# A graph network on one core: VectorE's order in the first two steps of a pair is changed

## The reference, cut to what matters

```python
h = x
for i in range(L):                                   # L = 4 layers
    hw = jnp.einsum('bnc,cd->bnd', h, weight[i])
    m = jnp.einsum('bjn,bjd->bnd', adj, hw)          # aggregation over the graph
    h = _gru_cell(m, h, w_ih[i], w_hh[i], b_ih[i], b_hh[i])
return layernorm(x + h * mask)                       # over the 128 channels
# _gru_cell: r, z = sigmoid(xr + hr), sigmoid(xz + hz); n = tanh(xn + r * hn)
#            h = (1 - z) * n + z * h
```

## Time and profile before

| what | value |
| --- | --- |
| median of 3 runs | 537.22 us (536.68 to 537.37) |
| the profiled execution: its own time | 537.31 us |
| its span from first to last instruction | 535.5 us |
| PE busy | 514.2 us, 96% of the span |
| DVE busy | 388.8 us, 73% |
| ACT busy | 383.8 us, 72% |
| POOL busy | 219.9 us, 41% |
| mean granted TensorE clock | 0.988 of full |

### The profile page before, as it was taken

The page is one execution under the profiler, slowest core; times in us unless marked ns, Lnnn a source line. Parts: engine busy times, 40 slices in busy tenths (PEclk is TensorE's granted clock), DMA queues, the critical chain, the costliest instruction groups (busy, mean ns, idle before and its releaser), DMA issues.

```text
span 535.5 us, 7420 instructions
## 1 busy us (share of the span) xinstructions
PE 514.2 (96%) x2288; PEld 422.0 (79%) x2288; DVE 388.8 (73%) x678; ACT 383.8 (72%) x638; POOL 219.9 (41%) x162
## 2 busy tenths in 40 slices
PE   5999999999999999999999999999999999999970
PEld 4688888888888888888888888888888888888760
DVE  3787666666788886666689886667688887767595
ACT  4668777648776779956786877984986777985444
POOL 2045232344345454432336644332355454344443
PEclk9999999999999999999999999999999999999995
DMA  8951653265642356273662166356472165424212
GB/s 305 380 199 47 226 195 126 87 169 156 234 141 80 121 179 226 88 224 119 203 239 77 61 211 215 118 163 190 133 280 80 60 218 171 171 89 151 86 60 82
DMA packets 78896, 85.13 MB, mean 159 GB/s; under 512 B 3768, under 2 KB 61712, under 8 KB 78864
## 3 DMA queue, kind: packets, MB, share of 16 engines
q1 hardware_dynamic: 78864, 84.73, 47.9%
HBM read 64.27 MB, written 20.45 MB: 158 GB/s over the span
## 4 chain that ended last, share of the span: by engine, by line
PE 91%; SPq 2%; DMA 1%; POOL 1%; DVE 1%; issue 1%; ACT 1%; POOLq 0%; DVEq 0%; ACTq 0%
PE p_S L508 40%; PE p_r L522 5%; PE p_r L518 5%; PE p_r L519 5%; PE p_z L518 5%; PE p_z L522 5%; PE p_z L519 5%; PE p_hn L518 3%; PE p_hn L522 3%; PE p_hn L519 3%; PE p_xn L522 3%; PE p_xn L518 3%; PE p_xn L519 3%; DMA adj_in<-in_adj_dram 1%; PE p_tr L453 1%
## 5 line engine op out<-in xcount | busy, mean ns | idle before, releaser
L1272 POOL TENSOR_TENSOR work<-hT,work 128x512 f32<-128x512 f32 x63 | 86.6, 1375 | 266.7 <-ACT work L710 266.7
L508 PE MATMUL p_S<-adj_hi,nat_hi 128*128 128x512 f32 x480 | 187.4, 391 | 0.0
L508 PE MATMUL p_S<-adj_hi,nat_lo 128*128 128x512 f32 x480 | 186.8, 389 | 0.0
L508 PEld LDWEIGHTS p_S<-adj_hi,nat_hi 128*128 128x128 f32 x480 | 90.1, 188 | 18.9 <-DVE nat_lo L894 0.3
L508 PEld LDWEIGHTS p_S<-adj_hi,nat_lo 128*128 128x128 f32 x480 | 90.1, 188 | 18.5
L1141 DVE SCALAR_TENSOR_TENSOR work<-p_hn,bias,work 128x512 f32<-128x512 f32 x62 | 46.5, 750 | 79.3 <-ACT work L710 78.8
L1276 POOL TENSOR_TENSOR work<-work 128x512 f32<-128x512 f32 x63 | 90.1, 1430 | 4.9
L710 ACT ACTIVATE work<-p_r,bsum 128x512 f32<-128x512 f32 x63 | 43.4, 688 | 60.7 <-PE p_r L522 60.6
L931 DVE STREAM_TRANSPOSE work<-hT 128x512 f32<-128x512 f32 x62 | 69.2, 1116 | 2.1
L710 ACT ACTIVATE work<-work,bias 128x512 f32<-128x512 f32 x63 | 45.7, 725 | 31.0 <-DVE work L1145 28.6
L682 ACT ACTIVATE low_words<-adj_in 128x1024 bf16<-128x1024 uint16 x64 | 67.1, 1049 | 1.0
(11 more groups left out here) (148 smaller groups left out, 924.8 us busy)
## 6 DMA issues: line engine op xcount, KB each, us to landing
adj_in<-in_adj_dram SPq DMA_DIRECT2D x72, 512.0 KB, 6.7
bounce<-work SPq DMA_DIRECT2D x62, 256.0 KB, 2.0
low<-bounce SPq DMA_DIRECT2D x62, 256.0 KB, 2.8
x_in<-in_x_dram SPq DMA_DIRECT2D x8, 512.0 KB, 6.7
y<-in_x_dram SPq DMA_DIRECT2D x8, 512.0 KB, 4.4
out_dram<-y SPq DMA_DIRECT2D x7, 512.0 KB, 4.1
out_dram<-y SPq DMA_DIRECT2D x2, 256.0 KB, 2.7
y<-in_L_gnn_w_ih_dram SPq DMA_DIRECT2D x2, 192.0 KB, 7.4
```

The lines of the kernel that those rows point to most:

```text
L508: last = nc.tensor.matmul(p_S[h][:, :], part[:, s, j], adj_hi[:, s, j, half(h)], start=(j == 0 and part is nat_hi), stop=(j == NB - 1 and ...
L1272: nc.gpsimd.tensor_tensor(t_sb[:, h], hT[:, s, half(h)], n_sb[:, h], ALU.subtract).then_inc(d_sub, 1)
```

## The change: what it does

Two edits in the list of VectorE. In steps 0 and 1 `take_xT` comes ahead of the `turn` of the step before (and behind its `new_state`). In step 0 of every pair but the first, `measure(p - 1, 0, 0)` comes ahead of `split_x(p, 1)` and of `s_low(p, 0, 1)`, where it was behind both. Nothing is added or left out, and no other engine's program is changed.

```diff
                     if g:
                         new_state(p, g - 1, 1)
+                    elif not first:
+                        new_state(p - 1, STEPS - 1, 1)
+                    if l == 0 and not (first and g == 0):
+                        take_xT(p, s)
+                    if g:
                         turn(p, g - 1, 1)
                     elif not first:
-                        new_state(p - 1, STEPS - 1, 1)
                         turn(p - 1, STEPS - 1, 1)
-                    if l == 0 and not (first and g == 0):
-                        take_xT(p, s)
                     s_low(p, g, 0)
...
+                    if g == 0 and not first:
+                        measure(p - 1, 0, 0)
                     if g == 0:
                         split_x(p, 1)
...
                     if not (first and g == 0):
                         s_low(p, g, 1)
                     if not first:
-                        if g == 0:
-                            measure(p - 1, 0, 0)
-                        elif g == 1:
+                        if g == 1:
                             measure(p - 1, 0, 1)
```

## The result

The changed kernel takes 536.27 us (median of 17 runs, 535.88 to 537.50), the kernel before 537.22 (median of 17, 536.46 to 539.18). The ratio is 0.9981, 95% interval 0.9973 to 0.9988: 0.95 us faster. Forecast were 536.2 us (range 535.7 to 537.3) and "within 0.2%"; it is 0.19%.

What follows compares the result with a forecast made beforehand. PE, 91% of the chain of waits, was taken as the bound. Removing 1.03 us of stalls, against 0 to 0.1 of small change, gives -1.0: 537.31 to 536.3 profiled, 536.2 as median, range 535.7 to 537.3.

Steps and rivals of the forecast that it cites:

- The ceiling: PE's stalls from step 0 to step 2 in three pairs, 0.41 + 0.16 + 0.46 = 1.03 us, are the most to win.
- Edit 1, step 0: take_xT ahead of the turn: DVE stands about 0.25 us, S_lo comes 0.3 to 0.4 us later, PE loses nothing.
- Edit 2: Step 0: statistics (0.78 us) fill DVE's gap before split_x; L1141 ends at 154.45 instead of 155.22, p_hn's stall goes.
- Edit 1, step 1: take_xT starts near 415.6 instead of 416.67, last pair's stall goes; the turn is 1.24 us later, costing nothing.
- The slower rival: Step 0's second half returns late if its DRAM trip takes over 7 us: +4.0 us, 541.2; chance 0.04, whole or part.
- The neighbour: Step 1: POOL's sum of x^T comes 1.1 us sooner; h_low may wait 0.6 us, no stall, 0.2 left.
- The first rival: h_low waits 1.4 us for a whole POOL operation; 0.2 to 0.3 per pair lost again, 536.8 us; chance 0.16.
- the late turn of step 7: Step 0's later turn of the pair before's state: residual two halves later, store behind first half's trip; costed at nothing.
- the second half's trip in step 1: Store and load through DRAM after the turn, 1.24 us later: 1.9 us of cover, otherwise up to 1.24 per pair.
- the signs that I had named: Right if p_hn never waits for L1141 nor p_r for hT_lo, and all pairs take 31.7 us from step 0 to 2.

Runs made afterwards that it cites:

- e1: Kernel before with only take_xT moved ahead of the turn in steps 0 and 1, statistics left where they were: 536.69 us, ratio 0.9991 to the kernel before.
- e5: Kernel before with step 0's four statistics issued a second time in their old place: 539.35 us, ratio 1.0035 to the kernel before.
- e6: Changed kernel with step 0's four statistics issued a second time in their new place: 536.47 us, ratio 0.9986 to the kernel before.
- e7: Changed kernel with step 1's turn of the second half put behind S_lo of half 0, h_low and S_lo of half 1: 539.03 us, ratio 1.0029.
- e8: Changed kernel with step 1's turn of the second half put behind L1147 and take_back of half 0: 559.66 us, ratio 1.0411 to the kernel before.
- e9: Changed kernel with POOL starting its sums of x^T in step 1 only when h_low has ended: 536.30 us, ratio 0.9981 to the kernel before.
- e3: Changed kernel measured again, unaltered, beside the other experiments: 536.38 us, ratio 0.9981 to the kernel before.
- e2: Kernel before with only step 0's statistics moved ahead of split_x, take_xT still behind the turn: 536.63 us, ratio 0.9989 to the kernel before.
- e12: e10 with S_lo of half 1 put ahead of the second half's residual in the last step: 536.22 us, ratio 0.9976 to the kernel before.
- e10: Changed kernel with SP's last two adjacency loads of step 7 issued behind the first turned half's store: 536.04 us, ratio 0.9979 to the kernel before.
- e11: e10 plus step 0's residual of the first half moved behind the second half's L1143 and L1147: 536.80 us, ratio 0.9985 to the kernel before.

## Why the prediction was right

**The ceiling.** PE bounds the pairs, and only its stalls could be won. I put them at 1.03 us; by the stall-free 31.77 they were 0.35 + 0.10 + 0.40 = 0.85 in the profiled execution, so the sum was 0.18 too high. The measured 0.95 (0.6 to 1.5 by the interval) agrees with either and can't confirm the one against the other. That the size came out so well means that nearly every stall goes in a typical execution. This is inferred: both profiles of the changed kernel are of slow executions and show one stall each, 0.9 and 0.49 us, and without it they would have taken 536.6 and 536.4, close to the medians.

**Edit 1, step 0.** The stand before take_xT was said to be 0.25 and is 0.27; S_lo was to be 0.3 to 0.4 later and is 150.48 - 150.17 = 0.3. What I missed is a small gain, 0.1 us at nat_lo through POOL's earlier end (e1).

**Edit 2.** The gap holds the statistics, nat_lo stays, L1143 ends 0.9 us sooner relative to PE. e5 and e6 show both sides: in the old place another 0.78 us of statistics cost PE 0.75 to 0.80 in each pair, in the new one they are nearly free.

**Edit 1, step 1.** e1 shows the last pair's stall gone. The turn's trip has 2.8 us of cover left (e7), so its 1.24 us later start costs nothing. The slower rival wanted a trip about 2 us longer than in the rows; none was seen for this half. What it costs when the cover does end is 0.55 us for 0.4 too late (e7) and 5.3 to 6.5 us per pair for waits of 3.3 to 4.1 (e8).

**The neighbour.** h_low was to wait up to 0.6 and waits 0.4; L1143 in step 1 hides it (e9). The first rival, a small wait that takes part back, named the wrong one.

**What I did not see.** I costed the late turn of step 7 at nothing and looked for danger in the second half's trip in step 1. By the signs that I had named, the last pair of the profiled execution came out wrong: p_r waits for hT_lo, p_hn once for L1143, and from step 0 to step 2 it takes 425.60 - (376.64 + 16.29) = 32.67 us. The trip that comes late is that of step 7's *first* half, whose store queues behind adjacency loads. The change does not move this trip, but edit 2 moves DVE towards it. In the last pair of the execution before, the load back was issued at 402.96, 9.75 us after step 0's start, and the residual found its block there:

```profile
406.20 0.69 DVE L1145 TENSOR_TENSOR work<-p_xn,work 128x512 f32<-128x512 f32 x1 [0.51 <-DVE work L1141]
406.81 1.13 DVE L947 SCALAR_TENSOR_TENSOR y<-low,mask,y 128x128 f32<-128x128 f32 x4
```

A block can be read about 3.0 us after its load back was issued (406.50 - 403.42 in the changed kernel, 155.75 - 152.72 in e3), so here at 406.0, 0.8 us before DVE came. With the statistics ahead DVE comes to the residual sooner: 12.62 us after step 0's start instead of 13.51 in the second pair (155.30 - 142.68, 156.01 - 142.50), 13.20 instead of 13.68 in the last; POOL's two operations come sooner by the same 0.9 and 0.5. In the last pair the trip was also 0.7 longer, 8.4 instead of 7.7. The block could be read there 13.57 us after step 0's start, and the kernel before began its residual 13.60 after it: in the old order even this trip would just have been in time. Over all profiles, the residual waits in none of the 9 pairs with the statistics in the old place (before, e1, e5), and in 5 of the 21 with them in the new place and store and residual where they were (changed kernel, e2, e3, e6, e8). So the term that I had at nothing is a price of edit 2. It was 0.5 to 0.9 us in three of these pairs (changed kernel, e3, e6), part of 0.46 in e2, and nothing in e8. This is read from profiles; no experiment made the trip late in the old order.

It cannot be all of the spread of the times. The kernel before spreads more, from 536.46 to 539.18, and the profiles up to e6 and e9 to e12 differ by up to 0.96 us already where step 2 of the first pair begins (48.48 in e1, 49.44 in e12), ahead of the three pairs that are treated here.

## What to carry to other kernels

Where one engine is busy almost without a break, sum its late starts before pricing a reordering of another: that sum is the ceiling, and here it was 0.2%. Then put movable work into the gap in front of an instruction that waits for something else, and check three times: the gap's length, the deadline behind it, and who else uses the memory path there. A cover is only known when the delay is measured from the consumer back through every idle time on the way, and the block that arrives latest need not be one that the change moves: work that is taken out of the way brings the reader nearer to a transfer that has not moved.

## What the runs showed of the hardware

- The load back behind a 256 KB store that follows six 512 KB loads in the same queue was issued 5.6 to 8.5 us after the store, and 2.8 to 4.8 us after it with two of the loads issued behind the store (e10 to e12); the median of all 62 such stores of the kernel before is 2.0 us to landing.
- Two-input VectorE instructions on on-chip memory stretch beside GpSimd's: one from 0.35 to 1.45 us, four from 1.13 to 3.34, while statistics and turns keep 0.85 and 1.1.
- TensorE stood still for 3.4 us and then ran at a granted clock of 0.50 (1.2 GHz) for about 3 us, until 1.00 came back (e8, second pair). After 3.05 us of standing still it fell to 0.50 as well, about 1 us after the start (e11). The wait of 1.2 us in the last step of the kernel before was followed by 1.00 as long as PE was busy, and all stretches from 50 to 500 us of that kernel have 1.00 in spite of its shorter stalls.
